# Sorting stage of a graph-network kernel: equal edges added on TensorE, one pass over numbers, two passes over equal edges, rows loaded ahead of the branch

## The reference

```python
h_self = x @ W_lin + b_lin
messages = x[dst] @ W_msg + b_msg                      # one row of x for each edge
msg_sum = segment_sum(messages, src, num_segments=12500)
counts = segment_sum(ones, src)
h_agg = msg_sum / max(counts, 1)
h = relu(concat([h_self, h_agg]) @ W_upd + b_upd)
out = layernorm(x + h)                                 # over the 128 numbers
```

## Time and profile before

| | us |
|---|---|
| median of three runs | 1358.66 (1356.97 to 1359.03) |
| profiled execution, its own time | 1359.65 |
| its span | 1357.9 |
| sorting stage, to the write of the flag | 450.6 |
| second half, from there to the end of the span | 907.3 |
| PE busy | 1203.5 (89%) |
| DVE busy | 996.9 (73%) |
| ACT busy | 681.1 (50%) |
| POOL busy | 633.6 (47%) |

### The profile page before, as it was taken

How to read it: one execution, slowest core, us unless ns; L and a number is a source line. 1 busy time by engine, 2 the same in 40 slices (tenths; PEclk the granted TensorE clock), 3 DMA queues, 4 the chain that set the end, 5 groups by cost and what they waited for, 6 DMA issues and landing times.

```text
span 1357.9 us, 42359 instructions
## 1 busy us (share of the span) xinstructions
PE 1203.5 (89%) x16556; PEld 742.2 (55%) x16556; DVE 996.9 (73%) x2602; ACT 681.1 (50%) x978; POOL 633.6 (47%) x673
## 2 busy tenths in 40 slices
PE   3869779689886399999999999999999999999996
PEld 2869678689885144444444444444444444444443
DVE  7999899999995556666666666666666666666665
ACT  1323323111101267666666666666666666666663
POOL 2000000000000477767777777777777777767772
PEclk9979779678786699999999999999999999999998
DMA  7333333243000545555554555455555555555531
GB/s 108 103 102 114 97 96 107 72 111 97 6 1 6 185 136 155 156 153 158 153 150 130 154 149 145 138 152 154 153 158 155 156 156 156 156 154 158 156 89 41
DMA packets 124987, 168.87 MB, mean 124 GB/s; under 512 B 34771, under 2 KB 93952, under 8 KB 124716
## 3 DMA queue, kind: packets, MB, share of 16 engines
q1 hardware_dynamic: 92226, 101.17, 23.1%
q0 software_dynamic: 31280, 64.23, 19.8%
q10 hardware_dynamic: 1290, 0.78, 0.3%
HBM read 142.91 MB, written 23.21 MB: 122 GB/s over the span
## 4 chain that ended last, share of the span: by engine, by line
PE 63%; DVE 28%; issue 4%; ACT 2%; DMA 1%; POOL 1%; DVEq 0%; SPq 0%; POOLq 0%; ACTq 0%
PE slot L1268 29%; PE acc L1282 20%; PE acc L1293 6%; DVE big L805 6%; DVE big L783 5%; PE slot L1318 2%; DVE big L835 2%; DVE big L842 2%; ACT big L573 2%; DVE big L841 2%; PE acc L1301 1%; PE acc L1159 1%; DVE big L1009 1%; PE slot L1309 1%; DVE big L790 1%
## 5 line engine op out<-in xcount | busy, mean ns | idle before, releaser
L573 ACT ACTIVATE big<-slot 128x768 bf16<-128x768 f32 x750 | 567.5, 809 | 311.3 <-PE slot L1268 311.3
L646 POOL DMA_INDIRECT big<-x,dst_at x500 | 481.4, 963 | 192.4 <-issue 73.3
L1268 PE MATMUL slot<-big 128*128 128x384 bf16 x2300 | 445.5, 328 | 32.8 <-ACT big L573 16.7
L950 DVE TENSOR_SCALAR big<-big,iota_k 128x512 bf16<-128x512 f16 x575 | 196.5, 371 | 281.3 <-PE slot L1268 267.8
L1268 PEld LDWEIGHTS slot<-big 128*128 128x128 bf16 x2300 | 189.9, 97 | 262.1 <-issue 137.8
L1282 PE MATMUL acc<-big 32*128 32x385 bf16 x6000 | 309.3, 324 | 0.0
L1282 PEld LDWEIGHTS acc<-big 32*128 32x128 bf16 x6000 | 124.0, 93 | 160.7 <-issue 110.6
L641 POOL MEMSET big<- 128x4 bf16 x6 | 0.3, 96 | 443.0 <-issue 443.0
L650 POOL DMA_INDIRECT big<-x,sp_i x150 | 144.9, 966 | 65.9 <-PE slot L1268 34.4
L960 DVE TENSOR_TENSOR big<-col_lo,iota_lo 128x512 bf16<-128x512 f16 x375 | 156.2, 417 | 0.0
L1159 PE MATMUL acc<-big,tri 125*125 125x100 f16 x1600 | 120.1, 241 | 8.2 <-DVE big L783 7.8
(11 more groups left out here) (148 smaller groups left out, 943.0 us busy)
## 6 DMA issues: line engine op xcount, KB each, us to landing
big<-rows SPq DMA_DIRECT2D x25, 1920.0 KB
x<-big SPq DMA_DIRECT2D x19, 480.0 KB, 3.1
big<-x,dst_at POOLq DMA_INDIRECT x500
big<-x SPq DMA_DIRECT2D x32, 192.0 KB, 2.4
big<-in_x SPq DMA_DIRECT2D x24, 256.0 KB
big<-base SPq DMA_DIRECT2D x24, 256.0 KB
out<-big SPq DMA_DIRECT2D x24, 256.0 KB, 5.4
big<-in_x SPq DMA_DIRECT2D x19, 320.0 KB, 4.5
```

Of the source, the lines that this page charges most:

```text
L573: act.activation(xg[n % NX][:, :, 0:F3], slot[z % 2][:, :, 0:F3], ACT.Copy).then_inc(s["xg_ready"], 1)
L646: pool.indirect_dma_start(out=xg_d[:, c, 0:F3], out_offset=None, in_=x3_dram, in_offset=bass.IndirectOffsetOnAxis(ap=dst_at[:, q, c:c + 1] ...
L950: last = nc.vector.tensor_scalar(W[R_ % NW_][:, k, :].rearrange("p (c h n) -> p c h n", c=4, h=4), brow[q % NB].rearrange("p (h c n) -> p ...
L1268: ins = nc.tensor.matmul(slot[z % 2][:, j, 0:F3], W[R_ % NW_][:, k, (c % 4) * P:(c % 4 + 1) * P], xwin[:, win_at(c) + k, :], start=k == 0, ...
```

## The change

Five edits:

1. **Equal edges on PE.** `add_ranks` gets one more matmul, of 40 columns, that adds `dupc` into the first of the five sums of `Q_ps`. `route` reduces straight into `r_all`; its addition is gone.
2. **Numbers scaled at once.** `lo1` and `dst1` stand side by side in one tile `nodes`, both are scaled by 1 or 1/512 (before: `lo1` by 256 or 1), so that one factor (the 511/512 one) and one SCALAR_TENSOR_TENSOR over 80 elements serve both. `decode` has seven instructions in place of ten, three of them over 1280 elements.
3. **Equal edges in two goes.** `prepare` runs for slab 0 (as before) and once for slabs 1 to 3 together, after `split_1(3)`; its tiles cover all chunks. It ends with a wait for its last sum and a semaphore increment; SP waits for two of these in place of four.
4. **Rows ahead of the branch.** SP issues `brow` of quads 0 and 1 after the window loads, as soon as all bins are filled and all rows are stored, and then waits for the flag.
5. **The largest rank** (the reduction over `r_all`) stands right behind `route(39)`, ahead of `decode(3)`.

```diff
@@ -126,20 +127,19 @@
-        def per_slab(n=2):
-            return [shaped(one_b.take(CS * T, f16), "p (c t) -> p c t", t=T) for _ in range(n)]
-        hi, lo1, dst1, dupc = [per_slab() for _ in range(4)]
-        same = [shaped(one_b.take(CS * T, f16), "p (c t) -> p c t", t=T) for _ in range(3)]
+        hi, dupc = [shaped(one_b.take(C * T, f16), "p (c t) -> p c t", t=T) for _ in range(2)]
+        nodes = shaped(one_b.take(2 * C * T, f16), "p (u v e) -> p u v e", v=2, e=2 * T)
-        red, s32, sa, sbb, s16, vlo, vdst = [one_b.take(2 * T, f16) for _ in range(7)]
+        s32, sbb, s16 = [one_b.take(2 * T, f16) for _ in range(3)]
+        val = shaped(one_b.take(4 * T, f16), "p (v e) -> p v e", v=2)
-        d_a, d_b, d_c, d_e = [shaped(one_b.take(CS * SL, i32), "p (c n) -> p c n", n=SL) for _ in range(4)]
+        d_a, d_b = [shaped(one_b.take(CS * 2 * SL, i32), "p (c v n) -> p c v n", v=2, n=SL) for _ in range(2)]
@@ -371,7 +374,7 @@
                 sp.wait_ge(base_stored[k], 16 * XB // 2)
-            sp.wait_ge(s["edges_ready"], NS)
+            sp.wait_ge(s["edges_ready"], 2)
 
@@ -384,19 +387,23 @@
 
+            def load_brow(q):
+                if q >= 2:
+                    sp.wait_ge(s["W_ready"], (q - 1) * RUNS)
+                rows = rows_dram[q * 4:q * 4 + 4, 0:CP, :].rearrange("h c n -> h (c n)").unsqueeze(0).to_broadcast([P, 4, CP * SL])
+                sp.dma_start(brow[q % NB].rearrange("p (h e) -> p h e", h=4), rows).then_inc(brow_loaded[q % NB], 16)
+
+
+            sp.wait_ge(s["T_made"], U)
+            sp.wait_ge(s["rows_stored"], 16 * NS)
+            load_brow(0)
+            load_brow(1)
+
             sp.wait_ge(s["flag_known"], 1)
...
             def fast():
-                sp.wait_ge(s["T_made"], U)
-                sp.wait_ge(s["rows_stored"], 16 * NS)
                 sp.wait_ge(s["lo_taken"], NS)
-
-                def load_brow(q):
-                    if q >= 2:
-                        sp.wait_ge(s["W_ready"], (q - 1) * RUNS)
-                    rows = rows_dram[q * 4:q * 4 + 4, 0:CP, :].rearrange("h c n -> h (c n)").unsqueeze(0).to_broadcast([P, 4, CP * SL])
-                    sp.dma_start(brow[q % NB].rearrange("p (h e) -> p h e", h=4), rows).then_inc(brow_loaded[q % NB], 16)
 
@@ -416,8 +423,6 @@
 
-                for q in range(NB):
-                    load_brow(q)
                 load_x4(0)
@@ -742,33 +747,38 @@
 
-            def prepare(k):
-
-                dve.wait_ge(edges_loaded[k], 32 if k < NS - 1 else 64)
-                b = k % 2
-                here = slice(k * CS, (k + 1) * CS)
-                sv_, dv_ = src_i[0:EP, here, :], dst_i[0:EP, here, :]
-                n = mark(nc.vector.tensor_single_scalar(m7[0:EP, :, :], sv_, P - 1, ALU.bitwise_and))
-                nc.vector.tensor_tensor(dst1[b][0:EP, :, :], dv_, bc(lowm1[0:EP, here], T), ALU.subtract)
-                nc.vector.memset(dupc[b][0:EP, :, 0:1], 0.0)
+            def prepare(c0, c1):
+
+                for k in range(c0 // CS, c1 // CS):
+                    dve.wait_ge(edges_loaded[k], 32 if k < NS - 1 else 64)
+                here, by_pair = slice(c0, c1), slice(c0 // 2, c1 // 2)
+                sv_, dv_, low7 = src_i[0:EP, here, :], dst_i[0:EP, here, :], m7[0:EP, 0:c1 - c0, :]
+                hi_, dup_ = hi[0:EP, here, :], dupc[0:EP, here, :]
+
+                def node(v):
+                    return nodes[0:EP, by_pair, v, :].rearrange("p u (c t) -> p u c t", c=2)
+
+                def pairs(a):
+                    return a.rearrange("p (u c) t -> p u c t", c=2)
+
+                n = mark(nc.vector.tensor_single_scalar(low7, sv_, P - 1, ALU.bitwise_and))
+                nc.vector.tensor_tensor(node(1), pairs(dv_), pairs(bc(lowm1[0:EP, here], T)), ALU.subtract)
+                nc.vector.memset(dup_[:, :, 0:1], 0.0)
                 after(n)
-                n = mark(nc.vector.tensor_tensor(hi[b][0:EP, :, :], sv_, m7[0:EP, :, :], ALU.subtract))
-                nc.vector.tensor_scalar(lo1[b][0:EP, :, :], m7[0:EP, :, :], 1.0, None, ALU.add).then_inc(s["edges_ready"], 1)
+                n = mark(nc.vector.tensor_tensor(hi_, sv_, low7, ALU.subtract))
+                nc.vector.tensor_scalar(node(0), pairs(low7), 1.0, None, ALU.add)
                 after(n)
-                sums = mark(nc.vector.tensor_tensor(dupc[b][0:EP, :, 1:T], hi[b][0:EP, :, 1:T], hi[b][0:EP, :, 0:T - 1], ALU.is_equal))
+                sums = mark(nc.vector.tensor_tensor(dup_[:, :, 1:T], hi_[:, :, 1:T], hi_[:, :, 0:T - 1], ALU.is_equal))
                 tests = [0, 0, 0]
...
                     if d < T:
-                        tests[d % 3] = mark(nc.vector.tensor_tensor(same[d % 3][0:EP, :, 0:T - d], hi[b][0:EP, :, d:T], hi[b][0:EP, :, 0:T - d], ALU.is_equal))
+                        tests[d % 3] = mark(nc.vector.tensor_tensor(same[d % 3][0:EP, 0:c1 - c0, 0:T - d], hi_[:, :, d:T], hi_[:, :, 0:T - d], ALU.is_equal))
                     if d > 2:
...
                         after(max(tests[e % 3], sums))
-                        sums = mark(nc.vector.tensor_tensor(dupc[b][0:EP, :, e:T], dupc[b][0:EP, :, e:T], same[e % 3][0:EP, :, 0:T - e], ALU.add))
-                return sums
-
-            def two_chunks(a, u):
-                k = 2 * (u % US)
-                return a[(u // US) % 2][0:EP, k:k + 2, :].rearrange("p c (a j) -> p (c a) j", j=2)
+                        sums = mark(nc.vector.tensor_tensor(dup_[:, :, e:T], dup_[:, :, e:T], same[e % 3][0:EP, 0:c1 - c0, 0:T - e], ALU.add))
+                after(sums)
+                dve.sem_inc(s["edges_ready"], 1)
 
@@ -810,25 +820,20 @@
                 dve.wait_ge(s["Q_added"], u + 1)
-                r2 = red[0:EP, :].rearrange("p (a j) -> p a j", j=2)
-                with nc.allow_low_precision("whole numbers below 2501 in fp16; 64 and over are told apart"):
-                    nc.vector.tensor_reduce(r2, Q_ps[b].rearrange("p (a h j) -> p a j h", h=NH, j=2), AX.X, ALU.add).then_inc(s["ranks_taken"], 1)
+                k2 = two_chunks(r_all, u)
+                with nc.allow_low_precision("whole numbers below 2521 in fp16; 64 and over are told apart"):
+                    nc.vector.tensor_reduce(k2, Q_ps[b].rearrange("p (a h j) -> p a j h", h=NH, j=2), AX.X, ALU.add).then_inc(s["ranks_taken"], 1)
                 dve.wait_ge(s["ranks_taken"], u + 1)
-                k2 = r_all[0:EP, 2 * u:2 * u + 2, :].rearrange("p c (a j) -> p (c a) j", j=2)
-                k = mark(nc.vector.tensor_tensor(k2, r2, two_chunks(dupc, u), ALU.add))
-                after(k)
 
...
                 k0 = mark(nc.vector.tensor_scalar(col(s32), k2, SL - 0.5, -float(SL), ALU.is_gt, ALU.mult))
-                k1 = mark(nc.vector.tensor_scalar(col(sa), k2, SL - 0.5, 255.0, ALU.is_gt, ALU.mult))
-                k3 = mark(nc.vector.tensor_scalar(col(sbb), k2, SL - 0.5, 511.0 / 512.0, ALU.is_gt, ALU.mult))
+                k1 = mark(nc.vector.tensor_scalar(col(sbb), k2, SL - 0.5, 511.0 / 512.0, ALU.is_gt, ALU.mult))
                 after(k0)
...
                 after(k1)
-                k1 = mark(nc.vector.scalar_tensor_tensor(out=col(vlo), in0=col(sa), scalar=1.0, in1=two_chunks(lo1, u), op0=ALU.add, op1=ALU.mult))
-                after(k3)
-                k3 = mark(nc.vector.scalar_tensor_tensor(out=col(vdst), in0=col(sbb), scalar=1.0 / 512.0, in1=two_chunks(dst1, u), op0=ALU.add, op1=ALU.mult))
+                k1 = mark(nc.vector.scalar_tensor_tensor(out=val[0:EP, :, :], in0=sbb[0:EP, :].unsqueeze(1).to_broadcast([EP, 2, 2 * T]), scalar=1.0 / 512.0,
+                                                         in1=nodes[0:EP, u, :, :], op0=ALU.add, op1=ALU.mult))
                 after(k0)
@@ -838,8 +843,9 @@
                 after(k0)
-                nc.vector.tensor_tensor(OHSV[b][0:EP, :, 0, :, :], OHS[0:EP, :, :, :], spread2(col(vlo), SL), ALU.mult)
-                nc.vector.tensor_tensor(OHSV[b][0:EP, :, 1, :, :], OHS[0:EP, :, :, :], spread2(col(vdst), SL), ALU.mult).then_inc(s["route_ready"], 1)
+                for v in range(2):
+                    ins = nc.vector.tensor_tensor(OHSV[b][0:EP, :, v, :, :], OHS[0:EP, :, :, :], spread2(col(val[:, v, :]), SL), ALU.mult)
+                ins.then_inc(s["route_ready"], 1)
 
@@ -847,23 +853,17 @@
                     dve.wait_ge(s["rows_stored"], 16 * k)
-                Tk = T_sl[k % 2]
-                a, b, c, e = [v[0:H, :, :] for v in (d_a, d_b, d_c, d_e)]
-                k1 = mark(nc.vector.tensor_copy(a, Tk[0:H, :, 0, :]))
-                k2 = mark(nc.vector.tensor_scalar(c, Tk[0:H, :, 1, :], 512.0, None, ALU.mult))
+                a, b = d_a[0:H, :, :, :], d_b[0:H, :, :, :]
+                n = mark(nc.vector.tensor_scalar(a, T_sl[k % 2][0:H, :, :, :], 512.0, None, ALU.mult))
+                after(n)
+                n = mark(nc.vector.tensor_single_scalar(b, a, 511, ALU.bitwise_and))
+                k1 = mark(nc.vector.tensor_single_scalar(a, a, 9, ALU.logical_shift_right))
+                after(n)
```

(27 more changed lines are left out.)

9 lines of the change are left out of this document (7 added, 2 removed).

## The result

The changed kernel takes 1343.66 us (median of 4 runs, 1341.12 to 1345.13), the kernel before beside it 1358.85 (1356.97 to 1360.19): a ratio of 0.9885, 95% interval 0.9872 to 0.9897. It is 15.2 us faster, where 25.7 were forecast, and its time lies outside the range of 1326 to 1341. The profiled execution took 1345.13 us with a span of 1343.4, at a mean granted clock of 0.954 (before 0.939).

What follows compares the result with a forecast made beforehand. DVE bounds the sorting stage and PE the second half; 12.6 + 5.2 - 0.3 + 1.3 + 0.3 + 1.6 + 5.0 = 25.7 us off 1359.65 gave 1333.9 profiled, 1333 median, range 1326 to 1341.

Steps and rivals of the forecast that it cites:

- Rows ahead of the branch: At the branch: early `brow` loads let DVE start 10.0 us earlier; POOL's gathers in quad 0 leave 5.0 us gained.
- Route: Sorting stage, DVE: 0.32 us saved in each of 40 units, 12.6 us in all (6.6 to 14.2).
- The matmul more: Sorting stage, PE: 40 added matmuls of 40 columns cost nothing, as PE has slack; uncovered 2.5 us.
- Prepare: Sorting stage, DVE: one preparation for slabs 1 to 3 instead of three, net 5.2 us saved.
- Waits for PE: DVE in the sorting stage: a 1.3 us rank-sum wait at unit 22 goes; the transposes' wait costs 0.3 more.
- rival A: Sorting stage: PE takes over from DVE, costing 6.3 us and the 1.3 us wait: 1341 us; chance 0.15.
- Largest rank: Ahead of the flag: the reduction moves into DVE's idle time before the last decode, 1.6 us saved.
- Decode: DVE's decode: seven instructions instead of ten, by four decodes 0.3 us saved.
- B: Quad 0: the gathers keep up and the 10.0 us come whole, 5 us more gained: 1328 us; chance 0.11.
- E: Ahead of the branch: SP is held, so the loads don't come early, 5 us less: 1338 us; chance 0.04.
- C: Quad 0: 24 gathers each wait for a DVE comparison, 8.4 us later in all: 1341 us; chance 0.02.
- D: Sorting stage: PE stays at half clock through units 4 to 39, slower than before: 1405 us; chance 0.03.

Runs made afterwards that it cites:

- the first experiment: The changed kernel with both loads of `brow` back behind the branch: 1342.74 us, ratio 0.9883 to the kernel before.

## Why the prediction was wrong

The failing step is *Rows ahead of the branch*, on both of its legs; one small term beside it, the waits for PE, did not come.

- **Route: right.** 0.31 us a unit instead of 0.32, 12.4 us in 40 units (forecast 12.6; 40 times 0.32 would be 12.8), and the product of 80 elements at the 0.15 assumed. *The matmul more* was costed at nothing, and in the units that is right: PE has gaps. But the step looked only at PE's time and not at its code. 80 instructions ahead of a dense run of 320 matmuls put a second fetch into it, 2.7 us (the first experiment), and it is in this run that nothing covers PE, since DVE waits for slab 3.
- **Prepare: right.** 25.1 to 20.1 us against 5.2 forecast.
- **Waits for PE: not gained.** I took a 1.3 us wait for gone with the preparation at unit 20. The run with four preparations has the same waits, so it was not the preparation's. In the changed kernel they are 7.9 us, 7.2 of them ahead of the last unit's `pick` and 0.7 behind it, instead of 7.3; forecast was 1.0 less. That rival A's mechanism (a shorter DVE unit leaves PE less room) adds to them is not shown: with the same code they are anywhere from 5.4 to 8.6. Of the 1.1 us that the table's first line misses these waits are 0.9.
- **Largest rank: right**, 1.6 us behind the laying. **Decode: nearly nothing**, from its first instruction to the laying 432.78 - 428.62 = 4.16 us before and 415.83 - 411.75 = 4.08 after, 0.1 of the 0.3 forecast. The second line misses 1.0 by this and by the 0.7 us of waiting for PE that stand there now, where DVE did not wait for PE before.
- **Rows ahead, first leg.** "So the first is there by 446, ahead of the flag": it was, but the loads were taken to cost nothing while they ran. At that place PE was laying slab 3 with its code coming over the same 16 DMA engines, and its block came 3.9 us later than its place in the laying asked for. The first experiment takes this away (5.78 to 2.48), and the run with the addition on DVE shows the loads nearly harmless (0.7 us) where the block comes ahead of their data, as does the run with rows ahead alone (none). So the second block alone costs 2.7 us and the loads alone up to 0.7, and together they cost 6.4: 3.7 by the loads where a block falls among them.
- **Rows ahead, second leg.** The prediction had the right candidate, POOL's gathers, and the right row: a gather that lands late beside a load of `brow`. It then held that load in its place in POOL's sequence, at the 25th of the 26 gathers. But SP sends it when DVE has made quad 0's tiles (`W_ready`), so it moves forward with DVE and not with POOL. DVE starts 10 us earlier against the gathers, the load meets the 21st gather instead of the 25th, where PE has five more to wait for, and the landing grew from 6.67 to 8.25 us. 1.2 us are left of 5.0. With the load held back it is 45.3 and 44.4 us from flag to quad 1, 6.6 and 7.5 less than before: at least the 5.0 forecast, but in a kernel that was not this one.

The rivals: B (no wait for gathers) and E (loads not early) did not come; the loads ran from 417 us on. C, gathers stretched by DVE, is not seen at its price: the first two gathers of quad 0 take 1.15 and 1.17 us beside DVE's first comparisons instead of 1.01 and 0.95 with DVE idle, as they do in every run here in which DVE starts early, and the other 24 take 0.94 to 0.99. That is 0.4 us in all where C had 8.4. The rule in the Trainium skill's "SBUF — State Buffer" may lie behind these two, which no run tests; it doesn't hold back the others. D did not come: the mean clock rose.

That the sum misses by 10.7 us of time and 11.2 of span is thus: 6.4 in the laying, 3.8 in quad 0 and 2.1 ahead of the laying (the table's first two lines), less 1.2 behind quad 1, which lie within the spread.

## What to carry to other kernels

A transfer that is sent earlier is not free where nobody waits for its data: ask what else uses the DMA engines at the new time, PE's own code included, and look in the profile for the "issue" standstills of dense runs of small matmuls. When one engine is let go earlier, list everything that its semaphores release (here a 1920 KB load) and move it in the forecast with that engine, against those that don't move. And an instruction added to PE far from the critical path can still shift a block boundary into it, so a change of 2 to 3 us at such a place should be checked there before it is put down to the edit.

## What was not expected of the hardware

- PE's code comes as packets of 16.4 KB over the same DMA engines as the data, one for every 128 matmuls with their weight loads. In these layings, at 11.5 ns from matmul to matmul (2.15 us for 187), each costs a standstill of 1.6 to 2.5 us, and PE goes on 2.1 to 3.3 us after the packet's start; beside two loads of 1920 KB that fill the engines (share 0.91 to 1.02) it was 5.78, and 5.77 in the run with four preparations. The Trainium skill's "DMA: Bandwidth & Descriptors", section "Queues, rings and completion order", lets a DMA engine go round between its queues packet by packet, typically 9 to 17 descriptors each. An estimate by it: 583 packets of q1 in the 6.2 us around the standstill (421.3 to 427.5), at 95% of 16 engines, are 0.16 us each, and 9 to 17 such would make 1.5 to 2.7 us if one of them is one descriptor; measured were 3.9.
- A gather issued beside one 1920 KB load was used 8.25 us after its issue, with the DMA engines 0.94 busy from 466 to 474 us; with the load held back the longest wait of PE fell from 5.9 us (6.6 in the changed kernel) to 2.1.
- The same programs ran at two speeds on different occasions, once at each speed on a chip of the same number (7): the kernel before at 1358 and at 1512 us, and the version with rows behind and held at 1340 and at 1487 to 1490. Of that one, the sorting stage is the same in both (last unit's `pick` at 397 to 399 us), the mean granted clock no lower (0.96 against 0.955), and matmuls and activations of the same length (327 and 809 ns). Only the second half is longer, about 41 us a quad, and there PE waits for ACT 60 us in all between 560 and 1300 us instead of 14. The cause is open. In that condition the version with the hold for quad 2 alone took 1002 us behind quad 1, and those with every load held 994; at the usual speed the hold gives nothing there (854.2 without, 855.6 with). That was not pursued.
